# A GNN and mixture-of-experts layer on one core: sort matmuls interleaved, table rows every second group, four more dense tiles, x1 reloads on ScalarE's queue

## The chip, the cores and the metric

The program runs on one core of a Trainium2 chip. The metric is the device time of one execution in microseconds (us), median of the runs. Engines are named as the profile names them: PE (TensorE matmuls) and PEld (its weight loads), DVE (VectorE), ACT (ScalarE), POOL (GpSimd), SP (SyncE, which here only issues DMAs). A "q" behind a name is that engine's sequencer issuing something.

## What is computed

A graph layer with 12,500 nodes of 256 features and 212,500 weighted edges, then a mixture of 8 experts of which each node uses 2:

```python
def _L0_gnn_ref(x, W, bias, edge_row, edge_col, edge_val):
    h = x @ W
    msgs = h[edge_col] * edge_val[:, None]
    return jax.ops.segment_sum(msgs, edge_row, num_segments=N_NODES) + bias

def _L0_ffn_ref(x, gamma, beta, Wr, br, W1, b1, W2, b2):
    xn = layernorm(x) * gamma + beta
    top_vals, top_idx = jax.lax.top_k(xn @ Wr + br, 2)
    w_full = softmax(top_vals) placed at top_idx
    for e in range(8):
        h = jax.nn.gelu(xn @ W1[e] + b1[e])
        y = y + (h @ W2[e] + b2[e]) * w_full[:, e]
    return y

x = x + _L0_gnn_ref(_layernorm(x), W, bias, src, dst, edge_weight)
x = x + _L0_ffn_ref(_layernorm(x), ...)
```

## The kernel before

Nodes are in 98 tiles of 128 rows. Each engine has its own program; they meet at semaphores, and every engine works strictly in the order written. The work has these stages.

1. **Counts and places** (0 to 390 us): for each tile of nodes, how many edges fall to it, and where each edge goes in a sorted list.
2. **Sort** (390 to 903 us): 64 groups of 26 columns of 128 edges. For group g, PE turns the digits of the edge places (`turn_digits`, L1776), multiplies them into distances in 7 parts (`distances`, L1785), ACT makes one-hots of each part by an exponential (`one_hots`, L917), DVE builds the values (`build`, L1342 to L1348), and PE spreads the 26 columns into the order of the list (`spread`, L1796, with four small matmuls of row numbers, L1801). The distances pass through two PSUM banks in turn, so PE may be at most two parts ahead of ACT. PE does distances(g) and then spread(g - 1). Every fourth group DVE (`records`) and ACT (`weights_of`) write a batch of 16 x 128 records, and POOL stores them with 16 indirect DMAs (`scatter`, L766). In POOL's program scatter(B) stands at group 4B + 6.
   Beside this, the table h of normalised x times W is made, one tile of rows at a time ("rows"). A step k of it is on PE L1720 and L1728 (`rows_of_h`), on ACT L861, L862, L867 and L851 (`rows`), on POOL L751 (`low_rows`, the low half of the 16-bit split) and two DMAs of SP. `step1`, `step2`, `step3` say at which points the 99 steps stand; `step3` holds the last 28 and puts them at groups 0 to 27 of the sort. Buffers are two deep: ACT's step for tile t waits until POOL has done `low_rows` of tile t - 2 and its store has landed (semaphores s_hhl and s_hst). low_rows(t) itself waits for ACT's step.
3. **Gather** (908 to 3345 us): POOL gathers rows of h for units of 8 x 128 edges (L798, 8 indirect DMAs each, 232 units), DVE makes targets (L1392 to L1403), PE sums them into the tile (L1832, L1834). After each tile follow layer norm, router and top-2. Tiles are "dense" or "routed". Sets of SB = 4 dense tiles (tiles 8c to 8c + 3, 12 sets, NSET) run through all 8 experts, one expert a step of the loop (`hidden`, L1885, 24 matmuls of 512 columns; `expert`, L1902, 48 of 256 columns), set c in steps 8c + 4 to 8c + 11; NEX = 96 such passes. The other 50 tiles (NR) are routed: ACT stores x1 (the rows so far) to `out` and the normalised rows to `z_rows`.
4. **Exchange** (3381 to 3478 us): SP reloads z rows (L691), POOL scatters each routed tile twice, once for each chosen expert (L815), in part 0 (the first R0 = 33 routed tiles) and later part 1. SP fills the ends of the experts' blocks with zeros (`fill_of`, L593 and L596, 9 DMAs) after DVE has set `zero_b` (L1648, L1649, which stand behind DVE's whole loop; s_rest), and then loads blocks (`load_block`, L703).
5. **Blocks** (3478 to 3917 us): NBL = NR + 2 x 8 = 66 blocks of 256 rows: `turn` (L1954), `first_layer` (L1970), `second_layer` (L1982, L1987), 54 matmuls in all for a block; ACT L1034, L1044, L1045; DVE L1663 to L1677; ACT stores the block to ys (L1052). From three blocks after the end of part 0 on, two routed tiles are combined with each block: POOL reloads x1 (L828, a plain DMA) and gathers two rows of ys for each node (L830), DVE combines (L1684, L1687), ACT stores to out (L1057).
6. **Tail** (3917 to 3980 us): the tiles of part 1 are combined the same way once all blocks are stored.

Of the kernel before, what the change touches and what calls it, by code (L numbers as in the profile page):

```python
# [5 lines left out]
def gnn_moe_layer_kernel(  # L6
# [115 lines left out]
    with ctx:  # L122
# [420 lines left out]
        step3 = {g: len(step1) + len(step2) + g for g in range(NT + 1 - len(step1) - len(step2))}  # L543
# [182 lines left out]
        def _(pool):  # L726
# [91 lines left out]
            for j in range(NR):  # L818
# [17 lines left out]
        def _(act):  # L836
# [113 lines left out]
            def transposed(t):  # L950
                act.wait_ge(s_tr, t + 1)
                reached(act, s_lgm, t - 1)
                q, c = t % (2 * SB), t // (2 * SB)
                dense = t not in place_of
# [34 lines left out]
            def store_set(c):  # L989
                act.wait_ge(s_yadd, SB * (quad(c * NE + NE - 1) + 1))  # L990
                if c == 0:
                    act.dma_start(out[0:P - PAD, :], acc[PAD:P, 0, 0, :]).then_inc(s_ost, 16)
                    r, q = P - PAD, 1
                else:
                    r, q = c * 2 * SB * P - PAD, 0
# [12 lines left out]
            for t in range(NT + SB - 1):  # L1008
# [11 lines left out]
                if t < NT:  # L1020
                    transposed(t)
                    if t % (2 * SB) == SB - 1 and t // (2 * SB) < NSET:
                        exps(t // (2 * SB))
# [56 lines left out]
        def _(dve):  # L1080
# [367 lines left out]
            def epilogue(t):  # L1448
                dense = t not in place_of
                q, c = t % (2 * SB), t // (2 * SB)  # L1450
# [15 lines left out]
            def x_low(t):  # L1466
                q, c = t % (2 * SB), t // (2 * SB)
# [4 lines left out]
            def top2(t):  # L1472
                dense = t not in place_of
                q = t % (2 * SB)
# [126 lines left out]
            def step(t):  # L1601
# [20 lines left out]
                if t < NT:  # L1622
# [5 lines left out]
                    elif t % (2 * SB) == SB - 1:  # L1628
                        differences(t // (2 * SB))
                        finalise(t // (2 * SB))  # L1630
# [14 lines left out]
            for t in range(NT + SB + 1):  # L1645
# [63 lines left out]
        def _(pe):  # L1709
# [69 lines left out]
            def distances(g):  # L1779
                pe.wait_ge(s_seen, slot_of_turn(g) + 1)  # L1780
                for j in range(NCH):
                    n, w = slot_of_part(g, j), width_of(j)
                    if n >= 2:
                        pe.wait_ge(s_seen, n - 1)
                    nc.tensor.matmul(slot(n)[:, 0:w * P], digits_T[:, g % 2, :],  # L1785
# [251 lines left out]
```

## Time and profile before

| | us |
|---|---|
| median of 3 runs (3973.16 to 3984.31) | 3982.83 |
| profiled execution | 3981.84 |
| its span, first to last instruction | 3979.7 |
| PE busy | 3194.3 (80%) |
| POOL busy | 2538.3 (64%) |
| DVE busy | 2415.8 (61%) |
| ACT busy | 1331.0 (33%) |

The span is 2.1 us shorter than the profiled execution's time, and that time is 1.0 us below the median. Busy shares are averages over six stages with different limits, so each stage has to be read by itself.

The views are read so. The table of stretches has, for each window in us, the busy time and the number of instructions of PE, PEld, DVE, ACT and POOL, PE's granted clock (1.00 is 2.4 GHz, 0.50 is 1.2 GHz), the DMA share and GB/s. A row of waits says who waited for whom, us in total, times, longest. A row of the groups has line, engine, operation, tiles, count, busy us and mean ns, then the idle time before them and what ended it. A row of the timeline has start us, us, engine, line, operation, tiles and count, with the idle time before it in brackets. A row of one line's instructions has count, shortest/median/longest ns, first and last start. A POOL row's DMA_INDIRECT is the making of one indirect DMA, not its transfer.

### The profile page before, as it was taken

The numbers are of one execution on the slowest core, as the hardware profiler recorded it, in microseconds if no ns is written. First come the engines' busy times: TensorE is split into PE (matmuls) and PEld (weight loads), VectorE is DVE, ScalarE is ACT, GpSimd is POOL, SyncE is SP. The second block draws the span as 40 slices with busy tenths as digits, with TensorE's granted clock in tenths as the row PEclk, the third lists the DMA queues.
The fourth block names the chain that finished last, engine by engine and source line by source line (L and its number), as shares of the span: only waits on it lengthen the run. The fifth ranks groups of instructions, "written<-read, shape, count | busy, mean of one in ns | idle before, by whom it ended". The sixth has DMA issues, their size and how long they took to land.

```text
span 3979.7 us, 75949 instructions
## 1 busy us (share of the span) xinstructions
PE 3194.3 (80%) x20888; PEld 2076.7 (52%) x20888; DVE 2415.8 (61%) x6037; ACT 1331.0 (33%) x2857; POOL 2538.3 (64%) x2491
## 2 busy tenths in 40 slices
PE   6677767824788899898988998998988989099983
PEld 4444444412455555555555555555555556088862
DVE  9699334514666666666666666676666665144563
ACT  1354656720222222222222222222222222066651
POOL 1241457877777777777777777777777776630264
PEclk9899989966899999999999999999999999599996
DMA  4341110003434334434343434343334346552463
GB/s 154 106 117 60 33 36 15 8 12 92 117 110 119 110 113 114 119 112 120 112 117 110 117 110 120 109 115 108 114 111 120 108 118 104 175 165 86 125 202 113
DMA packets 288427, 420.20 MB, mean 106 GB/s; under 512 B 89733, under 2 KB 218314, under 8 KB 288138
## 3 DMA queue, kind: packets, MB, share of 16 engines
q0 software_dynamic: 109280, 279.33, 25.2%
q1 hardware_dynamic: 112536, 72.81, 6.4%
q10 hardware_dynamic: 66324, 64.42, 5.1%
q8 instruction: 157, 2.57, 0.3%
q14 instruction: 130, 1.06, 0.1%
HBM read 339.36 MB, written 76.98 MB: 105 GB/s over the span
## 4 chain that ended last, share of the span: by engine, by line
PE 36%; DVE 14%; issue 11%; POOL 7%; DVEq 5%; DMA 2%; ACT 1%; SPq 1%; ACTq 0%; POOLq 0%
PE twin L1902 7%; PE twin L1832 6%; PE bank L1902 6%; POOL area L798 5%; DVE area L1395 3%; PE twin L1834 3%; DVEq L1410 2%; DVE area L1403 2%; PE twin L1885 2%; PE bank L1885 2%; PE twin L1970 2%; PE twin L1987 2%; POOL zs L815 2%; PE bank L1970 1%; PE bank L1987 1%
## 5 line engine op out<-in xcount | busy, mean ns | idle before, releaser
L798 POOL DMA_INDIRECT area<-h_table,listed x1856 | 1864.3, 1004 | 606.0 <-issue 542.9
L1832 PE MATMUL twin<-area 128*128 x2608 | 880.9, 385 | 76.7 <-POOLq L797 38.3
L1834 PE MATMUL twin<-area 128*128 x2608 | 718.2, 275 | 0.0
L973 ACT ACTIVATE area<-twin,b_t 128x512 f32<-128x512 f32 x192 | 132.0, 687 | 1446.0 <-PE twin L1885 860.2
L1403 DVE TENSOR_TENSOR area<-area,listed 128x1024 f16 x652 | 422.6, 689 | 106.9 <-DVE area L1395 94.9
L1832 PEld LDWEIGHTS twin<-area 128*128 x2608 | 257.0, 99 | 415.2 <-issue 183.3
L766 POOL DMA_INDIRECT edge_list<-area,didx x256 | 313.0, 1223 | 77.1 <-issue 77.1
L1902 PE MATMUL twin<-w2h,area 128*128 128x256 f16 x1536 | 338.6, 317 | 0.0
L751 POOL TENSOR_TENSOR area<-area 128x256 f16<-128x256 f32 x98 | 80.9, 829 | 339.8 <-ACT area L862 339.6
L1834 PEld LDWEIGHTS twin<-area 128*128 x2608 | 257.1, 99 | 49.1 <-issue 0.2
L1902 PE MATMUL bank<-w2h,area 128*128 128x256 f16 x1536 | 267.7, 273 | 0.0
L1785 PE MATMUL twin<-area 128*128 128x512 f16 (+1 forms) x448 | 173.0, 392 | 113.7 <-ACT area L909 65.9
L1392 DVE TENSOR_SCALAR rel<-listed,tile_no 128x8 f16 x326 | 77.8, 239 | 297.9 <-issue 251.0
L1510 DVE TENSOR_TENSOR area<-area 128x512 f16<-128x512 f32 x384 | 244.0, 688 | 17.2 <-ACT area L975 17.2
L1902 PE MATMUL twin<-w2l,area 128*128 128x256 f16 x768 | 243.7, 317 | 0.0
L1395 DVE TENSOR_TENSOR area<-pair_no,rel 128x1024 f16<-128x1024 f16 x326 | 225.7, 692 | 11.2
L917 ACT ACTIVATE area<-twin 128x512 f16<-128x512 f32 (+1 forms) x448 | 228.9, 565 | 5.5 <-PE twin L1785 5.2
L1885 PE MATMUL twin<-area,w1h 128*128 128x512 f16 x768 | 229.5, 380 | 0.0
L1885 PE MATMUL bank<-area,w1h 128*128 128x512 f16 x768 | 228.8, 380 | 0.0
L1851 PE MATMUL bank<-ident,zb 128*128 128x128 f32 x196 | 44.9, 316 | 207.7 <-DVE zb L1446 207.4
L1671 DVE TENSOR_TENSOR area<-area 128x512 f16<-128x512 f32 x132 | 91.4, 692 | 197.8 <-ACT area L1045 197.8
L828 POOL DMA_DIRECT2D area<-out_dram x50 | 29.3, 586 | 285.5 <-issue 220.6
(339 smaller groups left out, 6505.3 us busy)
## 6 DMA issues: line engine op xcount, KB each, us to landing
area<-h_table,listed POOLq DMA_INDIRECT x1856
area<-in_x_dram SPq DMA_DIRECT2D x194, 128.0 KB, 2.2
area<-zs SPq DMA_DIRECT2D x66, 256.0 KB, 2.9
ys<-area ACTq DMA_DIRECT2D x66, 256.0 KB
out_dram<-area ACTq DMA_DIRECT2D x100, 128.0 KB, 2.6
h_table<-area SPq DMA_DIRECT2D x97, 128.0 KB, 1.7
xt<-in_x_dram ACTq DMA_DIRECT2D x97, 128.0 KB
area<-in_L_ffn_W_dram ACTq DMA_DIRECT2D x16, 512.0 KB, 4.0
```

What stands on the lines that cost most here:

```text
L766: pool.indirect_dma_start(out=list_v, out_offset=bass.IndirectOffsetOnAxis(ap=didx[B % 4][:, j, r:r + 1], axis=0), in_=record[:, B % 4, j, ...
L798: pool.indirect_dma_start(out=stage[:, (k % RU) * UNIT + 2 * D * c:(k % RU) * UNIT + 2 * D * (c + 1)], out_offset=None, in_=h_table[:, :], ...
L917: nc.scalar.activation(ohs[:, g % 2, PER * j:PER * j + w, :].rearrange("p c s -> p (c s)"), slot(n)[:, 0:w * P], ACT.Exp, scale=SHARP).the ...
L973: nc.scalar.activation(h32[:, m, :], psH[m][:, :], ACT.Gelu, scale=1.0 / WSCALE, bias=b1_t[:, e * KH + m:e * KH + m + 1])
L1395: nc.vector.tensor_tensor(equal[:, :, :, :], pair_no[:, :, :].unsqueeze(1).to_broadcast([P, RUN // 2, P, 2]), rel[:, :].rearrange("p (j e) ...
L1403: made = nc.vector.tensor_tensor(target[:, ds((i % TR) * TGT + part * (TGT // 2), TGT // 2)].rearrange("p (j s e) -> p j s e", j=RUN // 2, ...
L1510: nc.vector.tensor_tensor(hl[:, i % 2, m, :], h32[:, m, :], hh[:, i % 2, m, :], ALU.subtract).then_inc(s_hl, 1)
L1785: nc.tensor.matmul(slot(n)[:, 0:w * P], digits_T[:, g % 2, :], rh[:, PER * j:PER * j + w, :].rearrange("p c s -> p (c s)"), start=True, st ...
L1832: nc.tensor.matmul(psA[:, :], target[:, ds(at, P, 2)], stage[:, ds(rows, 2 * D)], start=False, stop=False)
L1834: last = nc.tensor.matmul(psA[:, 0:D], target[:, ds(at + TGT // 2, P, 2)], stage[:, ds(rows, D)], start=False, stop=False)
L1885: last = nc.tensor.matmul(psH[m][:, :], a, r, start=(k == 0 and n == 0), stop=(k == KD - 1 and n == 2))
L1902: last = nc.tensor.matmul(half_bank(q), a, r[:, e, m, :], start=(m == 0 and n == 0), stop=(m == KH - 1 and n == 2))
```

## The change

Four edits. In the sort PE no longer does all 7 parts of the distances of group g and then all 26 columns of spread(g - 1); after each of the parts 1 to 6 it does four or five of those columns, and the four small matmuls (`places_of`) at the end. The last 28 table steps stand at the even groups 0, 2, ... 54 in place of 0 to 27. The last four tiles, 94 to 97, become a 13th dense set: 52 dense tiles, 104 passes, 46 routed tiles, R0 = 30, NBL = 62; the set's eight passes are steps 100 to 107 of the loop, behind the last tile. And the x1 reloads of the routed tiles go from POOL's queue to ACT's: the first four ahead of the blocks, each later one right behind the store of the tile four before it.

```diff
-    NSET = NT // (2 * SB)
+    begins = list(range(0, NT - 2 * SB + 1, 2 * SB)) + [NT - SB]
+    NSET = len(begins)
+    set_of = {b + q: (c, q) for c, b in enumerate(begins) for q in range(SB)}
-    routed = [t for t in range(NT) if t % (2 * SB) >= SB or t >= 2 * SB * NSET]
+    routed = [t for t in range(NT) if t not in set_of]
...
-        step3 = {g: len(step1) + len(step2) + g for g in range(NT + 1 - len(step1) - len(step2))}
+        step3 = {2 * k: len(step1) + len(step2) + k for k in range(NT + 1 - len(step1) - len(step2))}
...
-                p = routed[j] % 2
                 if j >= RX:
                     pool.wait_ge(s_o, j - RX + 1)
-                pool.wait_ge(s_xst[p], 16 * len([t for t in routed[:j + 1] if t % 2 == p]))
-                pool.dma_start(xr[:, j % RX, :], out_rows(routed[j])).then_inc(s_xr[j % RX], 16)
...
-            for t in range(NT + SB - 1):
+            for t in range(NEX + SB):
...
+            def load_x1(j):
+                p = routed[j] % 2
+                act.wait_ge(s_xst[p], 16 * len([t for t in routed[:j + 1] if t % 2 == p]))
+                act.dma_start(xr[:, j % RX, :], out_rows(routed[j])).then_inc(s_xr[j % RX], 16)
+
             def store_out(j):
                 act.wait_ge(s_o, j + 1)
                 act.dma_start(out_rows(routed[j]), ot[:, j % RX, :]).then_inc(s_ofin[j % RX], 16)
+                if j + RX < NR:
+                    load_x1(j + RX)
+
+            for j in range(RX):
+                load_x1(j)
...
-            def distances(g):
-                pe.wait_ge(s_seen, slot_of_turn(g) + 1)
-                for j in range(NCH):
...
+            def distance(g, j):
+                n, w = slot_of_part(g, j), width_of(j)
+                if j == 0:
+                    pe.wait_ge(s_seen, slot_of_turn(g) + 1)
+                if n >= 2:
+                    pe.wait_ge(s_seen, n - 1)
...
+            def spread(g, columns):
                 h, B, j = g % 2, g // BATCH, g % BATCH
-                pe.wait_ge(s_build, g + 1)
-                pe.wait_ge(s_seen, slot_of_part(g, NCH - 1) + 1)
-                for c in range(GC):
+                if columns[0] == 0:
+                    pe.wait_ge(s_build, g + 1)
+                    pe.wait_ge(s_seen, slot_of_part(g, NCH - 1) + 1)
+                    if j == 0 and B >= 2:
+                        pe.wait_ge(s_wrec, B - 1)
+                for c in columns:
...
+            between = [range(GC * k // (NCH - 1), GC * (k + 1) // (NCH - 1)) for k in range(NCH - 1)]
...
-                distances(g)
+                distance(g, 0)
+                for j in range(1, NCH):
+                    distance(g, j)
+                    if g >= 1:
+                        spread(g - 1, between[j - 1])
                 if g >= 1:
-                    spread(g - 1)
+                    places_of(g - 1)
                 if g in step3:
                     rows_of_h(step3[g])
-            spread(NGRP - 1)
+            spread(NGRP - 1, range(GC))
+            places_of(NGRP - 1)
...
-            for t in range(NT + SB + 1):
+            for t in range(NEX + SB + 1):
```

The rest of the diff replaces the arithmetic `t % (2 * SB)`, `t // (2 * SB)` by the lookup `set_of` and `begins` in ACT's, DVE's and PE's steps.

## Rows read from the trace of the kernel before

**Rows 1.** Table of stretches: first half of the sort, the gather, the exchange

```profile
425.00:630.00 205.00, 135.86 (x1005) 88.07 (x1006) 67.66 (x109) 118.95 (x317) 117.00 (x102) 0.87 0.12 33
...
904.00:3345.00 2441.00, 2144.30 (x13039) 1328.38 (x13040) 1593.00 (x4468) 615.32 (x1093) 1847.15 (x1839) 0.95 0.40 113
...
3390.00:3474.00 84.00, 0.00 (x0) 0.00 (x0) 5.68 (x6) 0.85 (x2) 59.67 (x60) 0.50 0.51 172
```

**Rows 2.** Waits of POOL's own instructions, 446 to 903.5 us

```profile
POOL area L751 <- ACT area L862: 54.7, 11, 8.1
```

**Rows 3.** Groups of POOL: 446 to 658, 658 to 821.5, 821.5 to 903.2 us

```profile
L766 POOL DMA_INDIRECT edge_list<-area,didx x96 | 117.2, 1220 | 28.4 <-issue 28.4
...
L766 POOL DMA_INDIRECT edge_list<-area,didx x96 | 133.5, 1391 | 29.1 <-issue 29.1
...
L766 POOL DMA_INDIRECT edge_list<-area,didx x64 | 62.4, 974 | 19.5 <-issue 19.5
```

**Rows 4.** Two lines of DVE's build: L1348 from 658 to 821.5 us, L1342

```profile
L1348 DVE TENSOR_TENSOR area<-area x32: 1872/1880/1887, 659.3 to 818.6; 128x3328 f16<-128x3328 f16 x32
...
L1342 DVE TENSOR_TENSOR area<-pair_no,area x64: 582/592/1012, 388.2 to 817.8; 128x832 f16<-128x832 f16 x64
```

**Rows 5.** Timeline of POOL: first and last scatter of the sort, and between

```profile
446.25 1.15 POOL L766 DMA_INDIRECT edge_list<-area,didx  x1 [0.19 <-issue]
...
469.49 1.30 POOL L751 TENSOR_TENSOR area<-area 128x256 f16<-128x256 f32 x2
...
481.35 1.48 POOL L751 TENSOR_TENSOR area<-area 128x256 f16<-128x256 f32 x1 [7.95 <-ACT area L862]
...
902.18 0.96 POOL L766 DMA_INDIRECT edge_list<-area,didx  x1 [0.31 <-issue]
```

**Rows 6.** Timeline of ACT: a group with a table step, one without

```profile
423.73 3.64 ACT L917 ACTIVATE area<-twin 128x512 f16<-128x512 f32 x7
...
430.93 0.61 ACT L917 ACTIVATE area<-twin 128x512 f16<-128x512 f32 x1
...
694.10 3.52 ACT L917 ACTIVATE area<-twin 128x512 f16<-128x512 f32 x7
...
699.20 0.60 ACT L917 ACTIVATE area<-twin 128x512 f16<-128x512 f32 x1
```

**Rows 7.** Timeline, end of the expert passes: PE, and DVE's clearing of zeros

```profile
3370.61 0.59 PE L1885 MATMUL twin<-area,w1h 128*128 128x512 f16 x2
...
3381.03 0.27 PE L1902 MATMUL twin<-w2h,area 128*128 128x256 f16 x1
...
3388.05 0.91 DVE L1649 MEMSET area<- 128x1024 uint32 x1 [0.16 <-issue]
```

**Rows 8.** Timeline of the exchange: POOL's first scatter, SP's fills, loads, first block

```profile
3381.39 1.00 POOL L815 DMA_INDIRECT zs<-area,slot_i  x1 [7.88 <-DMA area<-h_table,listed]
...
3458.62 9.16 SPq L593 DMA_DIRECT2D zs<-area  x8
...
3471.50 2.98 SPq L703 DMA_DIRECT2D area<-zs  x3
...
3477.80 0.61 PE L1970 MATMUL twin<-area,w1h 128*128 128x256 f16 x2 [2.39 <-DVE area L1665]
```

**Rows 9.** Table of stretches: blocks without and with tiles being combined

```profile
3540.00:3740.00 200.00, 196.88 (x1757) 169.89 (x1755) 99.74 (x195) 128.62 (x328) 0.00 (x0) 1.00 0.28 86
3765.00:3895.00 130.00, 106.74 (x924) 90.92 (x922) 79.94 (x165) 67.19 (x172) 76.31 (x86) 0.97 0.62 188
```

**Rows 10.** Timeline of POOL in the tail: its first and last x1 reload

```profile
3920.44 0.57 POOL L828 DMA_DIRECT2D area<-out_dram  x1 [48.97 <-DMA ys<-area]
...
3971.41 0.59 POOL L828 DMA_DIRECT2D area<-out_dram  x1
```

**Rows 11.** The line of ACT's stores to out

```profile
L1057 ACTq DMA_DIRECT2D out_dram<-area x50: 338/466/2122, 3767.3 to 3977.5; - x50
```

**Rows 12.** DMA issues of the page: the store of the table, us to landing

```profile
h_table<-area SPq DMA_DIRECT2D x97, 128.0 KB, 1.7
```

More of the change, by code:

```diff
@@ L952, in transposed @@
                 reached(act, s_lgm, t - 1)
-                q, c = t % (2 * SB), t // (2 * SB)
-                dense = t not in place_of
+                dense = t in set_of
+                c, q = set_of.get(t, (0, 0))
                 if dense:
@@ L994, in store_set @@
                 else:
-                    r, q = c * 2 * SB * P - PAD, 0
+                    r, q = begins[c] * P - PAD, 0
                 act.dma_start(out[r:r + (SB - q) * P, :].rearrange("(q p) d -> p q d", p=P),
@@ L1021, in _ @@
                     transposed(t)
-                    if t % (2 * SB) == SB - 1 and t // (2 * SB) < NSET:
-                        exps(t // (2 * SB))
+                    if t in set_of and set_of[t][1] == SB - 1:
+                        exps(set_of[t][0])
             store_set(NSET - 1)
@@ L1448, in epilogue @@
             def epilogue(t):
-                dense = t not in place_of
-                q, c = t % (2 * SB), t // (2 * SB)
+                dense = t in set_of
+                c, q = set_of.get(t, (0, 0))
                 rows = acc[:, c % 2, q, :] if dense else accr[:, t % 2, :]
@@ L1466, in x_low @@
             def x_low(t):
-                q, c = t % (2 * SB), t // (2 * SB)
+                c, q = set_of[t]
                 dve.wait_ge(s_xTh, t + 1)
@@ L1472, in top2 @@
             def top2(t):
-                dense = t not in place_of
-                q = t % (2 * SB)
+                dense = t in set_of
+                c, q = set_of.get(t, (0, 0))
                 biggest, which = (mx[:, q, :], ix[:, q, :]) if dense else (mxr[:, :], ixr[:, :])
@@ L1777, in turn_digits @@
                                  start=True, stop=True).then_inc(s_made, 1)
-            def distances(g):
-                pe.wait_ge(s_seen, slot_of_turn(g) + 1)
-                for j in range(NCH):
[L1782 to L1785, printed above, removed]
-                                     rh[:, PER * j:PER * j + w, :].rearrange("p c s -> p (c s)"), start=True,
-                                     stop=True).then_inc(s_made, 1)
-            def spread(g):
-                h, B, j = g % 2, g // BATCH, g % BATCH
-                pe.wait_ge(s_build, g + 1)
-                pe.wait_ge(s_seen, slot_of_part(g, NCH - 1) + 1)
-                if j == 0 and B >= 2:
-                    pe.wait_ge(s_wrec, B - 1)
-                for c in range(GC):
+            def distance(g, j):
[4 more added lines that the diff above has]
+                    pe.wait_ge(s_seen, n - 1)
+                nc.tensor.matmul(slot(n)[:, 0:w * P], digits_T[:, g % 2, :],
+                                 rh[:, PER * j:PER * j + w, :].rearrange("p c s -> p (c s)"), start=True,
+                                 stop=True).then_inc(s_made, 1)
+            def spread(g, columns):
+                h, B, j = g % 2, g // BATCH, g % BATCH
+                if columns[0] == 0:
[4 more added lines that the diff above has]
+                for c in columns:
                     nc.tensor.matmul(ps_out[B % 2][:, j * NF * Q:(j + 1) * NF * Q], ohs[:, h, c, :],
@@ L1798, in spread, with places_of @@
                                      stop=(c == GC - 1))
+            def places_of(g):
+                h, B, j = g % 2, g // BATCH, g % BATCH
                 for r in range(RQ):
@@ L1906, in weights_T @@
             def weights_T(c):
-                t = c * 2 * SB + SB
+                t = begins[c] + SB
                 pe.wait_ge(s_wf, c + 1)
@@ L1926, in _ @@
             pe.wait_ge(s_clear, 1)
-            for t in range(NT + SB + 1):
+            for t in range(NEX + SB + 1):
                 i = t - SB
```

6 lines of the change are left out of this document (3 added, 3 removed).

## The prediction

> **What bounds the kernel now.** I read the stretches of the timeline first, because the whole-span shares hide that every stage has another limit, and then the waits and the timeline of the engine that each stretch points to.
>
> The gather is 2441 of 3980 us. POOL is busy 1847 us of it with the making of indirect DMAs [rows 1], with 0.3 us of issue before each as in the sort [rows 5]; it never rests for long, and the change doesn't touch it. So its length is taken as it is, and the ends are what counts: when it starts and what is left behind it.
>
> It starts when the last scatter of the sort has landed, so the sort ends with POOL: last call at 902.18 [rows 5], though PE, ACT and DVE finish their groups at about 825. In the first half POOL has 117 busy us in 205 [rows 1]. It waits 54.7 us, in 11 waits, for ACT's table step [rows 2]. The timeline shows why: a batch of 16 scatters starts at 446.25, low_rows follow at 469.49, and the low_rows that stands ahead of the next batch starts only at 481.35 after 7.95 us of waiting [rows 5]. It is a ring. low_rows is queued behind 16 scatters, ACT's step two tiles on waits for it, the groups behind that step wait too, and the next batch waits for the groups. In the second half nothing waits but POOL is full: 96 calls take 133.5 busy and 29.1 idle [rows 3], 1.69 us each. After the groups end, a call takes (62.4 + 19.5) / 64 = 1.28 us [rows 3]. The 39.7 us by which 96 calls are longer fall on 32 builds of DVE [rows 4], 1.24 us each.
>
> Behind the gather, PE has nothing to do from 3390 to 3474 and its clock is at 0.50, 1.2 GHz [rows 1]: it waits for POOL's scatters of part 0 and then SP's fills and loads [rows 8]. Then come 66 blocks, bound by PE (196.9 of 200 us busy, [rows 9]), and a tail bound by POOL [rows 10].
>
> **Part 1, the sort.** What the change gives here I sum as POOL's own time. When does POOL start? Now a group with a table step takes 430.93 - 423.73 = 7.20 us and one without 699.20 - 694.10 = 5.10 [rows 6]. ACT's exponentials are 3.52 of it, the rest is ACT waiting until PE has done the spread. With the columns between the parts that wait goes: PE's 26 columns and 7 parts fit beside ACT's exponentials. The nearest rows give the bounds for a group without a table step: 3.52 us (the exponentials alone) and today's 5.10; I take 4.1, near the lower, because each part must still pass from PE to ACT. For one with a step, 6.5 (7.20 is the bound above). Before the first batch stand six groups; three lose their table step (3 x 3.1) and three gain 0.7: 446.25 - 11.4 = 435.
>
> From there on I have to ask whether POOL still waits. A step at every second group halves the demand, and two tiles back now means four groups back. ACT's step at group 4B + 6 needs only the low_rows ahead of scatter(B - 1), which is done before that batch starts; the first step that needs one behind scatter(B - 1) is that of group 4B + 8. So scatter(B) is ready some 15 us after scatter(B - 2) ends (0.65 of low_rows, a store that lands 1.7 us after its issue [rows 12] and ACT's step, about 4 us; then two groups of 10.6 us together), while scatter(B - 1) keeps POOL busy for 25 us. The ring is open with 10 us to spare, and POOL is full from 435 on. The sum: 435 + 256 calls x 1.28 (328) + 57 builds x 1.24 (71) + 12 pairs of low_rows x 1.4 (17; 1.30 a pair [rows 5], and 0.1 at the handover) = 851. Today 903: 52 us less. In bounds: 35 less if the groups keep 7.2 and 5.1 and clock dips cost more, 60 less if builds that now fall in POOL's waits cost nothing. Note what this says of the interleaving: it only brings the start forward. The groups need about 22 us a batch, POOL 28; even at 24.6 (two of each kind as today) POOL would be the bound.
>
> The columns add no wait of their own: the build and the last exponential of group g - 1 are done one group earlier than they are asked for. Table stores end at group 54, long before 851. The gather starts 52 us earlier, with everything behind it.
>
> **Which price a build has is where the Trainium skill comes in.** Calls beside builds are 0.42 us longer on average [rows 3], and I take 1.24 us for a build. The Trainium skill, page "SBUF — State Buffer", section "Who interferes with whom", says that VectorE and GpSimd share one pair of ports, that a VectorE instruction with two SBUF inputs can hold off GpSimd, and that the loser is blocked for the whole instruction. This is a rule against packing builds beside scatters; what it would give here is the third rival.
>
> **Part 2, the thirteenth set.** It adds eight passes. hidden of the last pass starts at 3370.61, expert of the last at 3381.03 [rows 7]: one pass is 10.42 us of PE at full clock. Eight are 83.4, and weights_T with b2_terms add about 2, a clock dip or two 2 more: 87.4. They stand where PE was idle. But DVE's zeros (done at 3388.96, [rows 7]) stand behind its whole loop, and SP's fills wait for them. They were covered: fills started only at 3458.62, after SP had fed POOL's scatters of part 0 [rows 8]. Part 0 is now 60 scatters and not 66: 3381.4 + 60 x 1.28 = 3458, no longer last. Zeros are now done at 3388.96 + 87.4 = 3476.4, which is late next. From the first fill to the first block's matmul there are 3477.80 - 3458.62 = 19.2 us [rows 8], all in series: nine fills, landing, load, turn. So the first block starts at 3476.4 + 19.2 + 0.3 = 3495.9: 18 us later than now. Bounds: 14 (fewer clock dips) and 27 (clock at half for a while, or the set's exponentials and table loads holding up passes at steps 97 and 98).
>
> **Blocks.** 54 matmuls a block: 1757 / 54 = 32.5 blocks in 200 us, 6.15 each, and 924 / 54 = 17.1 in 130, 7.60 each, while tiles are combined [rows 9]. Part 0 has three tiles fewer, so of four blocks saved two are of each kind: 2 x 6.15 + 2 x 7.60 = 27.5.
>
> **Part 3, reloads on ACT.** A DMA issue costs ACT 0.34 to 0.47 us [rows 11]. While tiles are combined ACT's last store waits for DVE's last combine and the next gelu waits for that store, so ACT is on the path. The first of two reloads fits into ACT's wait for the second combine; the second adds 0.45 to each of 15 blocks: 6.8 us. Bounds: 0, and 15 if both count. The first four reloads (1.7 us) stand beside SP's fills. In the tail POOL starts its x1 reloads (3971.41 - 3920.44) / 16 = 3.19 us apart [rows 10], two gathers and a reload to a tile. Without the reload two gathers take 2.56, and there are 16 tiles, not 17: 16 x 2.56 = 41.0 against 16 x 3.19 + 3.4 = 54.4. That is 13.4 less; the last landing, combine and store stay. Bounds: 8 and 15.
>
> **Sum**, against the profiled execution's 3981.8: -52 + 18 - 27.5 + 6.8 - 13.4 = -68.1, so 3913.7, and 1.0 more for the median: 3914.7, say 3915.
>
> **Rivals.** *The ring stays closed (the slower side).* If ACT's step at group 4B + 6 still depended on a low_rows behind the previous batch, for instance because the store of that tile lands late, each of 12 batches would have a gap of about 13.4 us (16 scatters end at 469.5, the next batch begins at 483) and not 1.4, and there were five such gaps till now. That is 144 us more, less some 26 for builds that fall into the gaps: 3915 + 118 = 4033. It decides at a gap of 7 us a batch (3915 + 12 x 5.6 = 3982). Against it speak the 10 us of room. Chance 6%.
>
> *Only part of it.* ACT and PE don't get from 7.2 and 5.1 to less, clock dips and record batches fall together, and POOL is left with gaps of 4 us, or a build costs more. The sort then gives 25 us and not 52, and the first block is 25 us late and not 18: 3915 + 27 + 7 = 3949. Chance 14%.
>
> *A build blocks POOL for its whole length.* A build's long step is 1.88 us, with its first step of 0.59 [rows 4] it would be 2.47 and not 1.24: 57 x 1.23 = 70 more, 3985, no faster than now. By the rule named above this is what would come. The trace has 32 builds at 1.24, so 3%.
>
> *The blocks or the tail take back the gain* (ACT's queue holding its gelus up by more than both issues, as the 2.1 us of the longest store [rows 11] would): 15 blocks x 1.7 = 25 more than reckoned, 3940. Chance 7%.
>
> **How the numbers follow.** The forecast case has 70%. Its own range is the bounds together, not all at one end: 3897 to 3936. Reaching to the two partial cases gives 3896 to 3950; outside are the closed ring, the blocked POOL and some of each tail. A measurement of this kernel can tell 0.3%, 12 us. Faster by more than that: 70 + 14 + 7 less 3 for what the two partial cases may come to = 88%. Within 0.3%: 5%. Slower: 7%.
>
> **What would show it.** In the changed profile: no waits of POOL L751 for ACT L862 beyond a few us between the first and last scatter; first scatter near 435, last near 851; in a group without a table step the L917 starts 4.1 us apart; PE busy at full clock from 3390 - 52 on for some 85 us; nine fills starting right behind DVE's zeros, not behind the scatters; first block 18 us later counted from the first gather; 62 blocks, 8.05 us each while tiles are combined; gathers of ys in the tail 1.28 us apart with nothing between. I am wrong if POOL has gaps in the sort, if passes without a tile take much more than 10.4 us, or if ACT's store and reload pairs spread the blocks further.

## The result and the profile after

| | before | after |
|---|---|---|
| median, us | 3983.57 (4 runs) | 3913.78 (4 runs, 3908.99 to 3914.66) |
| profiled execution, us | 3981.84 | 3912.91 |
| its span, us | 3979.7 | 3911.1 |
| POOL busy, us | 2538.3 (64%) | 2494.5 (64%) |

The kernel before is the one run beside it. After divided by before is 0.9828, 95% interval 0.9809 to 0.9846: 69.8 us less. 3915 was forecast. Seven of the twelve experiments below ran where the kernel before took 5333 to 5362 us, its gather above all being slower; their totals tell little, and only their stages are read. The span cut at the points which the prediction named:

| stretch | before | after | difference | predicted |
|---|---|---|---|---|
| start to first gather | 907.9 | 855.7 | -52.2 | -52 |
| first gather to the first block's matmul | 2569.9 | 2580.5 | +10.6 | +18 |
| first block's matmul to the last of all | 439.3 | 422.6 | -16.7 | -20.7 |
| last matmul to the end | 62.6 | 52.3 | -10.3 | -13.4 |
| sum | 3979.7 | 3911.1 | -68.6 | -68.1 |

The first term and the sum are right to half a us; the three terms behind it are off by 3 to 7 us, one in the change's favour and two against it. The rows now. First the table of stretches after (us, then busy us and instructions of PE, PEld, DVE, ACT, POOL, clock, DMA share, GB/s): the sort, the added passes, blocks without and with tiles being combined.

```profile
425.00:630.00 205.00, 147.55 (x1292) 101.58 (x1291) 98.52 (x150) 147.83 (x380) 166.20 (x133) 0.89 0.11 27
3330.00:3414.00 84.00, 83.69 (x593) 58.19 (x590) 36.25 (x68) 35.28 (x56) 57.52 (x58) 1.00 0.42 139
3500.00:3700.00 200.00, 196.77 (x1753) 169.40 (x1752) 100.61 (x197) 127.80 (x326) 9.70 (x10) 1.00 0.30 93
3702.00:3831.10 129.10, 100.56 (x810) 83.26 (x810) 71.14 (x146) 58.93 (x151) 46.58 (x49) 0.92 0.58 173
```

POOL's busy time in the same 205 us of the sort went from 117.00 [rows 1] to 166.20. The passes keep PE busy for 83.69 of 84 us at full clock. While tiles are combined, 810 matmuls at 54 a block are 15 blocks in 129.1 us, 8.61 each (7.60 in [rows 9]).

The waits of POOL after, 430 to 855 us (us in total, times, longest):

```profile
POOL edge_list L768 <- issue: 74.7, 247, 0.3
POOL area L753 <- ACT area L861: 8.7, 1, 8.7
```

The waits of [rows 2] are gone but for one, which ends before the first scatter. The timeline of POOL shows the same at the places of [rows 5]: first scatter, low_rows directly between two batches, last scatter, first gather.

```profile
428.79 1.48 POOL L753 TENSOR_TENSOR area<-area 128x256 f16<-128x256 f32 x1 [8.72 <-ACT area L861]
430.45 1.16 POOL L768 DMA_INDIRECT edge_list<-area,didx  x1 [0.18 <-issue]
...
455.24 1.76 POOL L768 DMA_INDIRECT edge_list<-area,didx  x1 [0.30 <-issue]
457.02 1.32 POOL L753 TENSOR_TENSOR area<-area 128x256 f16<-128x256 f32 x2
458.50 1.15 POOL L768 DMA_INDIRECT edge_list<-area,didx  x1 [0.16 <-issue]
...
850.03 0.96 POOL L768 DMA_INDIRECT edge_list<-area,didx  x1 [0.31 <-issue]
855.73 0.98 POOL L800 DMA_INDIRECT area<-h_table,listed  x1 [4.74 <-SPq L677]
```

The first twelve batches start 27.2 to 28.1 us apart, with 1.5 us between the last call of one and the first of the next. ACT's exponentials, to be held against [rows 6]:

```profile
685.89 3.52 ACT L916 ACTIVATE area<-twin 128x512 f16<-128x512 f32 x7
...
691.85 3.64 ACT L916 ACTIVATE area<-twin 128x512 f16<-128x512 f32 x7
696.10 3.52 ACT L916 ACTIVATE area<-twin 128x512 f16<-128x512 f32 x7 [0.29 <-PE twin L1794]
705.66 0.38 ACT L860 ACTIVATE area<-bank 128x256 f16<-128x256 f32 x1 [6.04 <-DMA h_table<-area]
```

A group with a table step is 691.85 - 685.89 = 5.96 us, one without 4.25. Then ACT waits 6 us for a store whose low_rows stand behind the batch in POOL's order: once in four groups ACT waits for POOL, and POOL no longer for ACT. From the 17th to the 52nd the groups start about 11.0, 6.0, 6.0 and 4.3 us apart in turn, together POOL's 27.3 a batch.

### The profile page after: what moved, and what is told of

It is laid out like the page before. It is cut to its first block, busy times and chain, and to the rows that moved or that the text cites. A ratio compares the mean times of both kernels' runs of the same rounds, so it can differ in the third digit from the quotient of the medians.

```text
span 3911.1 us, 76490 instructions
## 1 busy us (share of the span) xinstructions
PE 3228.5 (83%) x21249; PEld 2117.9 (54%) x21249; DVE 2439.0 (62%) x6051; ACT 1362.3 (35%) x2894; POOL 2494.5 (64%) x2425
## 4 chain that ended last, share of the span: by engine, by line
PE 43%; DVE 16%; issue 9%; DVEq 5%; POOL 3%; DMA 1%; ACT 1%; ACTq 0%; SPq 0%; POOLq 0%
PE twin L1922 9%; PE bank L1922 7%; PE twin L1852 7%; DVE area L1404 4%; PE twin L1854 3%; PE twin L1905 3%; PE bank L1905 3%; DVEq L1419 2%; POOL area L800 2%; PE twin L1990 2%; DVE area L1412 2%; PE twin L2007 2%; PE bank L1990 2%; PE bank L2007 1%; DVE rel L1401 1%
## 5 line engine op out<-in xcount | busy, mean ns | idle before, releaser
L972 ACT ACTIVATE area<-twin,b_t 128x512 f32<-128x512 f32 x208 | 142.9, 687 | 1468.6 <-PE twin L1905 821.8
L768 POOL DMA_INDIRECT edge_list<-area,didx x256 | 326.4, 1275 | 76.2 <-issue 74.7
L1922 PE MATMUL twin<-w2h,area 128*128 128x256 f16 x1664 | 355.2, 311 | 0.0
L829 POOL DMA_INDIRECT area<-ys,back_i x92 | 89.3, 971 | 334.4 <-DMA ys<-area 260.4
L1519 DVE TENSOR_TENSOR area<-area 128x512 f16<-128x512 f32 x416 | 266.7, 689 | 48.9 <-ACT area L974 48.9
L1922 PE MATMUL bank<-w2h,area 128*128 128x256 f16 x1664 | 289.5, 273 | 0.0
L1922 PE MATMUL twin<-w2l,area 128*128 128x256 f16 x832 | 258.3, 310 | 0.0
L1905 PE MATMUL twin<-area,w1h 128*128 128x512 f16 x832 | 247.9, 380 | 0.0
L1905 PE MATMUL bank<-area,w1h 128*128 128x512 f16 x832 | 247.6, 379 | 0.0
L1922 PE MATMUL bank<-w2l,area 128*128 128x256 f16 x832 | 226.9, 273 | 0.0
```

Of the source, the lines that this page charges most:

```text
L768: pool.indirect_dma_start(out=list_v, out_offset=bass.IndirectOffsetOnAxis(ap=didx[B % 4][:, j, r:r + 1], axis=0), in_=record[:, B % 4, j, ...
L1519: nc.vector.tensor_tensor(hl[:, i % 2, m, :], h32[:, m, :], hh[:, i % 2, m, :], ALU.subtract).then_inc(s_hl, 1)
L1905: last = nc.tensor.matmul(psH[m][:, :], a, r, start=(k == 0 and n == 0), stop=(k == KD - 1 and n == 2))
L1922: last = nc.tensor.matmul(half_bank(q), a, r[:, e, m, :], start=(m == 0 and n == 0), stop=(m == KH - 1 and n == 2))
```

## What the experiments showed

**Which edit gives what.** Four kernels did one edit each on the kernel before, whose median beside them was 3977.55 (19 runs).

*Only the interleaving* (`distance`, `spread(g - 1, between[j - 1])` and `places_of` as in the diff of the change; the table steps left at groups 0 to 27).

> The kernel before with only the spread columns put between the parts of the distances; table steps at groups 0 to 27, 12 sets, reloads on POOL. My theory (the ring of low_rows, ACT's step and scatter limits the first half, POOL the second): the ring stays closed, with five waits of POOL; the groups get about 1.2 us shorter, so the first scatter comes some 7 us earlier and each of the five gaps of 13.4 us shrinks to about 10; last scatter near 880 (903 before), time 20 to 24 us less. Rival (the interleaving is what frees POOL): last scatter near 851, 50 us less. Rival (POOL full anyway in the second half): only the first scatter's 7 us.

Measured: 3972.21, ratio 0.9986 (0.9977 to 0.9996), 5.3 us less. First scatter 436.7 (446.25 before), last ending at 894.2 (903.1): what was won ahead of the first scatter, 9.6 us, was kept (8.9), and nothing more. Its waits of POOL, 436 to 895 us:

```profile
POOL edge_list L766 <- issue: 76.7, 255, 0.3
POOL area L751 <- ACT area L862: 49.5, 11, 7.7
```

Eleven waits, as before, with 49.5 us and not 54.7: faster groups don't open the ring, and what its waits lost, 5.2 us, the calls took back: they are 69.5 us over 0.97 each in all, and 64.7 before, since more of them stand beside builds. I had written 20 to 24 us less and was wrong; the prediction's own sentence, that interleaving "only brings the start forward", was right.

*Only the rows.*

```diff
-        step3 = {g: len(step1) + len(step2) + g for g in range(NT + 1 - len(step1) - len(step2))}
+        step3 = {2 * k: len(step1) + len(step2) + k for k in range(NT + 1 - len(step1) - len(step2))}
```

> The kernel before with only the last 28 table steps at groups 0, 2 ... 54. My theory: this alone opens the ring. POOL is full from the first scatter (about 440, three of six groups at 5.1 us and not 7.2) to the last near 857; gaps between batches 1.5 us and not 13.4; time some 46 us less. A group pair takes 12.3 us, 24.6 a batch, which is less than POOL's 27. Rival (PE and ACT must be faster too, or else the ring only moves): gaps of 5 us and more stay, last scatter at 880 or later.

Measured: 3936.51, ratio 0.989 (0.9873 to 0.9906), 41.0 less, last scatter ending at 858.9. So this one line opens the ring. I had expected groups of 24.6 us a batch and gaps of 1.5 us; the groups take 7.2 and 6.5 us in turn, 27.4 a batch, and there are 3.9 us between POOL's batches of 23.4: the groups are the bound, at the same 27.3 us a batch at which POOL is when both edits are made. Added to this line, the interleaving brings the first scatter from 439.3 to 430.4 and the last from 858.9 to 851.0, and moves nothing between.

*Only the thirteenth set* (`begins`, `set_of`, loops to NEX + SB).

> The kernel before with only the thirteenth dense set. My theory, with the sizes that the changed kernel showed: first block 10 us later counted from the first gather, 62 blocks and not 66 (27.5 us less), the 4.8 us stall at the tenth block gone, one tile less in the tail (3.2 us less): 25 us less, about 3958. Rival (the stall's end belongs to another edit): 20 us less.

Measured: 3958.18, ratio 0.9941 (0.9924 to 0.9957), 19.4 less. First block 2584.4 us after the first gather, against 2569.9: 14.5 later, and not 10. From it to the last matmul there are 408.2 us, 31.1 less: four blocks, and the step from the ninth block to the tenth, 6.2 us and not 10.9. So the end of that stall belongs to this edit. I had expected 25 us less in all.

*Only x1 on ACT's queue.*

> The kernel before with only the x1 reloads on ACT's queue. My theory as the changed kernel showed it: each of 17 blocks with tiles being combined takes 1.0 us more (8.6 and not 7.6), the 17 tiles of the tail 0.6 us less each: 17 - 10 = 7 us MORE, about 3990. Theory of the prediction (0.45 us a block): 7.6 - 10 = 3 us less, about 3981.

Measured: 3988.3, ratio 1.0019 (1.0009 to 1.0028): 10.8 us more by the medians, 4 to 11 by the interval. Alone this edit is a loss. Its own part is nearer to 7, as expected: in the profile 3.4 of 10.8 us more lie ahead of the first gather, which the edit doesn't touch, while first block to last matmul takes 13.5 more and the rest 6.4 less. The stretches with tiles being combined, of the set alone (reloads on POOL) and of this kernel (on ACT), columns as above:

```profile
3759.90:3875.00 115.10, 95.50 (x811) 81.06 (x812) 71.20 (x146) 59.20 (x151) 65.81 (x75) 0.96 0.63 190
```

```profile
3766.60:3912.80 146.20, 117.66 (x918) 96.34 (x919) 79.91 (x164) 66.92 (x171) 52.81 (x55) 0.89 0.56 170
```

15 blocks at 7.67 us and 17 at 8.60: the edit costs 0.93 us a block (0.96 against the 7.64 of the same 17 blocks before), two issues of 0.47 us [rows 11]. Both count.

By the medians the four edits alone come to 54.9 us less, and together they gave 69.8. By the stages of the profiles, counting for each edit those that it touches, they nearly add up: sort -8.9 and -44.2, first block +14.5, blocks -31.1 and +13.5, tail -3.2 and -6.4, which with 0.3 in e4's gather is -65.5 against -68.6. Most of the rest is the gather's own length (2467.9 us of calls in e3_set_only, 2463.6 in the changed kernel). So no edit needs another one to be worth what it is.

**x1 reloads on SP's queue.** The changed kernel with

```diff
-                act.dma_start(xr[:, j % RX, :], out_rows(routed[j])).then_inc(s_xr[j % RX], 16)
+                sp.dma_start(xr[:, j % RX, :], out_rows(routed[j])).then_inc(s_xr[j % RX], 16)
...
+                for j in combined_by(n - 5):
+                    if j + RX < NR:
+                        sp.wait_ge(s_o, j + 1)
+                        load_x1(j + RX)
```

The lower lines stand behind SP's load of block n; the first four reloads behind its first block loads.

> The changed kernel with the x1 reloads of the routed tiles on SP's queue instead of ACT's (the first four behind the loads of the first blocks, each later one behind a block load). Theory (both issues of ACT count in every block in which tiles are combined, 1.0 us together): these blocks go from 8.5 back to 7.6 us, 15 blocks, so 14 to 15 us less than the changed kernel: 3899, ratio to the kernel before about 0.979. Rival (a block is 8.5 us for another reason, such as POOL's gathers now being back to back): blocks stay at 8.5 and the time at 3914. In the tail the distance from the last combine to the end stays near 5.4 us by the theory that POOL's own end is last there, and falls to 2 to 3 us if it is ACT's queue.

The total, 5328.6 against 5332.59, ratio 0.9981 (0.9948 to 1.0015), tells nothing. In the stage, the 15 blocks with tiles combined took 8.23 us each, and 8.87 in e7_build_in_4 and 8.95 in e6_zeros_early beside it with reloads on ACT. Where the kernel before took 3978 us, the same edit, with others ahead of the blocks, gave 7.61 (e13, below), with POOL's gathers still back to back: so the gathers aren't what made these blocks longer. From the last gather of the tail to the end there were 9.3 us, exactly as with reloads on ACT (3901.87 to 3911.1): so not ACT's queue but POOL ends last.

**The zeros early.** DVE's two clearings moved from behind its loop to its step NT + 4:

```diff
+                if t == NT + 4:
+                    dve.wait_ge(s_idle, 1)
+                    nc.vector.memset(zero_b, 0.0)
+                    nc.vector.memset(b2_z, 0.0).then_inc(s_rest, 1)
```

> The changed kernel with DVE's two clearings that the fills wait for moved from behind DVE's loop into its step 102, before the last passes of the experts end. Theory (DVE's place in the order is what ends last ahead of the fills): the first fill starts some 60 us earlier, as soon as SP is done with the scatters' reloads, and the first block starts when the next late thing lets it, which I take to be DVE's weights and ACT's exponentials behind the loop, or PE's own last pass: 3425 instead of 3436, 11 us less, 3903. Rival (the chain fills, landing, load, turn is not what the first block waits for): nothing changes, 3914.

Total 5321.61 against 5332.59, ratio 0.9977 (0.9943 to 1.001). As expected, 11.8 us went: first block at 4813.9, 10.6 us behind PE's last pass, where the changed kernel has 22.4 (3413.8 to 3436.2). The timeline of DVE and PE shows what is late next:

```profile
4810.23 2.33 DVE L1672 TENSOR_TENSOR area<-area 1x2048 f16<-1x2048 f32 x1
4812.59 0.43 DVE L1676 CAST area<-area 128x512 f16<-128x512 f32 x1
4813.06 0.69 DVE L1678 TENSOR_TENSOR area<-area 128x512 f16<-128x512 f32 x1
...
4813.89 0.60 PE L1994 MATMUL twin<-area,w1h 128*128 128x256 f16 x2 [10.19 <-DVE area L1678]
```

The split of b2, 5 us of DVE behind its loop, stands ahead of the first block's cast. That was never on the path before, since fills were later.

**Both, and all of the preparation early.** x1 on SP, the clearings at step 102, weights and b2 at 107, ACT's exponential and table load at 101. It was run three times.

> The changed kernel with x1 reloads on SP's queue and with all preparation of the blocks early: DVE's clearings at its step 102, the weights and b2 at 107, ACT's exponential and table load at 101. Theory: 15 us from the reloads, 11 us from the clearings and up to 8 more as the first block then waits for PE's last pass and its own load alone (3417): 3880 to 3888. Rival (the early instructions take DVE's or ACT's time from the last passes): the passes stretch by 3 to 5 us and the time is 3890 to 3900.

Measured: 5306.71 against 5332.59, ratio 0.9959 (0.9928 to 0.999). First block 3.8 us behind the last pass, the passes not stretched.

> The kernel of e8_sp_and_early once more, since its chip took 5333 us for the kernel before, over a thousand more than the others, with runs 80 us apart, so that only stages could be read there. From those stages: first block 3.8 us behind the last pass of PE and not 22.4 (18.6 less), blocks with tiles combined 8.1 us and not 8.7 (9 to 15 us less in all). On a chip like that of the changed kernel's runs that is 3914 - 18.6 - 12 = 3883. Rival (what is won ahead of the blocks is given back in the first ten, where SP's queue mixes block loads and reloads of z): 3895 to 3905.

Measured: 5307.82 against 5362.27, ratio 0.9906 (0.9874 to 0.9938); again 3.8 us.

> The kernel of e9_sp_and_early_again a third time, since all comparisons after the first ran where the kernel before took over 5330 us. Where it takes about 3980 the theory gives 3914 - 18.6 (first block 3.8 us and not 22.4 behind the last pass of PE) - 14.5 (15 blocks with tiles combined at 7.64 us and not 8.61) = 3881, first block 22 to 24 us earlier against the first gather's start than 2580.5, no more than 2563; the end still 9.3 us behind the last gather's issue. Rival (the first blocks give it back, as in e8 and e9, where the blocks 2 to 5 took 46 us and not 25): 3900. Where the kernel before takes over 5300 us again: ratio 0.99 to 0.996 as before, and nothing new.

Measured: 3883.91, kernel before 3978.38, ratio 0.9759 (0.9743 to 0.9776). It is faster than the changed kernel by about 0.7%, the two intervals lying apart, and its profiled span is 30.1 us shorter (3881.0). First block 2561.9 us after the first gather, 18.6 earlier, the term of the expectation's sum and not the 22 to 24 that it also names. Its first block and the stretch with tiles combined:

```profile
3418.12 0.39 PE L2004 MATMUL twin<-area,w1h 128*128 128x256 f16 x2 [3.34 <-DVE area L1688]
```

```profile
3687.70:3801.80 114.10, 93.96 (x810) 80.29 (x810) 70.80 (x146) 58.94 (x151) 47.80 (x49) 0.97 0.65 195
```

15 blocks at 7.61: 15.0 us less than at 8.61. But the tenth block began 12.9 us behind the ninth and not 6.2, which gives back 6.7. What holds it up is SP's queue: the tenth block's load stands behind five rounds of three z rows, one z row and nine fills; here it went out 51.9 us behind the first block's matmul, and 48.2 in the changed kernel (52.3 before). SP, here first and then the changed kernel:

```profile
3415.45 2.77 SPq L712 DMA_DIRECT2D area<-out_dram  x4
...
3470.01 5.03 SPq L706 DMA_DIRECT2D area<-zs  x5
```

```profile
3484.41 12.18 SPq L705 DMA_DIRECT2D area<-zs  x6
```

The four first x1 reloads, 2.8 us of SP, stand ahead of these rounds, and the blocks start sooner against them. That these are the reasons is read from the order; neither was tried alone.

**What a build costs a scatter.** In the changed kernel's trace, DVE and POOL in the same stretch:

```profile
604.32 1.89 DVE L1357 TENSOR_TENSOR area<-area 128x3328 f16<-128x3328 f16 x1
607.51 0.59 DVE L1351 TENSOR_TENSOR area<-pair_no,area 128x832 f16<-128x832 f16 x1 [1.30 <-PE twin L1814]
...
608.33 1.87 DVE L1357 TENSOR_TENSOR area<-area 128x3328 f16<-128x3328 f16 x1
```

```profile
603.07 0.97 POOL L768 DMA_INDIRECT edge_list<-area,didx  x1 [0.31 <-issue]
604.34 2.70 POOL L768 DMA_INDIRECT edge_list<-area,didx  x1 [0.30 <-issue]
607.35 0.96 POOL L768 DMA_INDIRECT edge_list<-area,didx  x1 [0.30 <-issue]
608.62 2.42 POOL L768 DMA_INDIRECT edge_list<-area,didx  x1 [0.31 <-issue]
```

The call of 604.34 ends at 607.04, the build's at 606.21; the call of 608.62 at 611.04, the build's at 610.20: 0.84 us after it, and so do all 54 calls of the trace that start while L1357 runs (0.83 to 0.85). A call that is undisturbed takes 0.97 us, so it has 0.13 us behind it when it is stopped and then does the rest. Calls that started up to 0.18 us before the build were held too in the kernel before, those that started 0.25 us or more before it were not. The shorter L1351 (L1342 before) holds calls the same way:

```profile
433.07 0.59 DVE L1351 TENSOR_TENSOR area<-pair_no,area 128x832 f16<-128x832 f16 x1 [3.33 <-PE twin L1814]
```

```profile
433.19 1.32 POOL L768 DMA_INDIRECT edge_list<-area,didx  x1 [0.30 <-issue]
```

L1351 ends at 433.66 and the call at 434.51, 0.85 us behind it. But it is short: 15 calls of this trace lost 1.7 us to it together, 24 calls before lost 6.3. A call comes every 1.28 us, so the wait for L1357 would be its length less half of that if they met at random, an estimate: 1.88 - 0.64 = 1.24. That this is the price read from [rows 3] is in part chance. Of the time lost there 4.6 us are the short instruction's and 36.1 the long one's, 1.13 a build; in the changed kernel the long one took 76.3 us for 56 builds, 1.36 each.

If so, shorter pieces should cost less. First four in a row:

```diff
-                nc.vector.tensor_tensor(rhs[:, h, :, :, :, :], ...)
+                for i in range(4):
+                    a, b = GC // 2 * i // 4, GC // 2 * (i + 1) // 4
+                    ins = nc.vector.tensor_tensor(rhs[:, h, a:b, :, :, :], ...)
```

> The changed kernel with the build's 1.88 us instruction cut into four of about 0.5 us each, the same work. Theory (a call of POOL that starts while such an instruction runs is held until this instruction ends, so that its price is its length less about half a call's period, 1.24 us): four short pieces let calls in between, the price falls to 0.3 to 0.6 us a build, the last scatter ends at 805 to 820 instead of 851, and the time is 30 to 45 us less: 3870 to 3885. Rival A (POOL stays out until all pieces have ended): last scatter at 851, time 3914. Rival B (the price is a matter of the bytes that DVE moves, not of the length of one instruction): each piece costs a quarter, the sum stays, 851.

Total 5343.05 against 5332.59, ratio 1.0001 (0.9969 to 1.0033). Last scatter ending at 864.9, and at 860.4 and 857.1 in two kernels beside it without the cut (e5_x1_on_sp, e6_zeros_early). So rival A holds: POOL stays out until all pieces have ended. DVE and POOL at one build:

```profile
537.29 2.08 DVE L1360 TENSOR_TENSOR area<-area 128x768 f16<-128x768 f16 x4
```

```profile
537.58 2.63 POOL L768 DMA_INDIRECT edge_list<-area,didx  x1 [0.30 <-issue]
```

Four pieces of 0.55 us take 2.08, so each begins before the last has ended, and the call ends at 540.21, 0.84 us behind the fourth. Then the same pieces apart, on top of the kernel with all preparation early:

```diff
+                    if i:
+                        dve.wait_ge(s_seen, slot_of_part(g, 2 * i - 1) + 1)
```

> The kernel of e9_sp_and_early_again with the build's instruction cut into four, of which the second, third and fourth each wait for ACT's exponential of the parts 1, 3 and 5 of the same group, so that they stand about 1.2 us apart; in e7_build_in_4 the four followed each other so closely (each started before the one before had ended) that they held POOL as one of 2.1 us. Theory (a call that reaches its port while such an instruction runs waits until it ends, then needs 0.84 us more; so a lone piece of 0.55 us costs 0.55 / 1.28 x 0.55 / 2 = 0.12 us on average): the price of a build falls from 1.24 to about 0.5, 57 x 0.75 = 43 us less, last scatter at 808 to 815 instead of 851, time 38 to 43 us below that of e9. Rival A (what counts is the work that DVE does in all, not how long it holds on without a break): last scatter at 851 or later, time as e9. Rival B (the later end of the build makes PE wait for it and the groups slow down): groups above 5.5 us each, last scatter between 820 and 860.

```profile
538.67 0.69 DVE L1367 TENSOR_TENSOR area<-area 128x1024 f16<-128x1024 f16 x1 [2.31 <-issue]
...
541.70 0.55 DVE L1367 TENSOR_TENSOR area<-area 128x768 f16<-128x768 f16 x1
```

```profile
538.79 1.42 POOL L783 DMA_INDIRECT edge_list<-area,didx  x1 [0.30 <-issue]
540.51 0.97 POOL L783 DMA_INDIRECT edge_list<-area,didx  x1 [0.30 <-issue]
541.78 1.31 POOL L783 DMA_INDIRECT edge_list<-area,didx  x1 [0.30 <-issue]
```

The rule holds for single pieces (539.36 to 540.21, 542.25 to 543.09: 0.85 and 0.84), and the price fell: all 256 calls together were 15 us over 0.97 us each, and 81 in e9_sp_and_early_again, without the spacing. Most batches took 20.5 to 21.5 us. Yet the last scatter ended at 926.7 and the time was 5364.09 against 5362.27, ratio 0.9981 (0.9935 to 1.0027), 56 above e9. POOL's waits, 430 to 927 us:

```profile
POOL area L768 <- ACT area L877: 117.5, 14, 13.1
```

Rival B, and more than it: groups took some 8 us, and POOL waits for ACT's table step again.

> The kernel of e11_build_apart once more. On its chip the price of a build did fall (from 73 us over all calls to 15), but the last scatter came at 927, since groups took 8 us and more: ACT's exponentials started up to 2.2 us after they could have, where in the changed kernel's own trace they never waited over 0.4 us for PE; in the same chip's run without the spacing they waited up to 1.6. Theory (that delay belongs to that chip, whose kernel before took 5362 us): on a chip where the kernel before takes about 3980, the groups stay below 5.5 us, last scatter at 805 to 825, time 3914 - 19 (early preparation) - 12 (reloads on SP) - 30 to 40 (price of builds) = 3843 to 3855. Rival (the loop is in the order: DVE waits for ACT, PE for DVE): groups 6.5 us and more on any chip, last scatter 880 to 930, time 3910 to 3960. On the slow chip again: as e11_build_apart.

Measured: 5337.51 against 5334.81, ratio 1.0011 (0.9978 to 1.0043), last scatter ending at 928.0, as in the run before. It fell again on a slow kernel before, so whether the order itself (DVE waits for ACT's parts, PE for the build) slows the groups, or only there, stays open. What is shown is the price of a build, and that this way of lowering it isn't free.

## Why the prediction was right, point by point

**Sort, -52 predicted, -52.2.** The mechanism is shown: the ring opened, and rows alone open it. The start was 430.4 and not 435, because a group is 5.96 and not 6.5 with a table step (4.25 and not 4.1 without). From there on the trace gives 851.0 - 430.4 = 420.6 against 328 + 71 + 17 = 416. The calls together are 79 us over 0.97 us each, which makes 1.38 and not 1.24 for each of 57 builds, low_rows with handovers take 17 us as reckoned, and calls and issues by themselves 325 and not 328. The start came 4.6 us early and the rest was 4.6 us longer, so that the two meet at 851 is luck to that extent. One aside was wrong: "even at 24.6 POOL would be the bound". Without interleaving the groups take 27.4 (e2), since one without a step then takes 6.5 and not 5.10.

**Build beside scatter.** The third rival is out: 1.38 us a build with its short instruction, not 2.47. But the Trainium skill's rule (page "SBUF — State Buffer", section "Who interferes with whom", that the loser is blocked for the whole instruction) agrees with the rows: each call waits to the build's very end. My reading of it for the rival was wrong, not the rule: the price isn't the length but the length less the part that runs before a call gets there, for the short L1351 too. The same section holds, as inferred, that an instruction with two inputs leaves the making of descriptors alone; the 54 calls here say otherwise, and the measurement decides.

**First block, +18 predicted, +10.6.** The failed step is the term of the passes, "87.4". Zeros ended 79.5 us later against the first gather. From there to the first block it is 19.9 us, 19.5 predicted. Of the eight passes seven came 10.4 or 10.5 us behind the one ahead of them and one 12.5, at a clock of 1.00, without the dip allowed for. They took 85.6 us, 1.8 less than reckoned. What I didn't see is that the last passes of the kernel before weren't clean: `hidden` of the 94th, 95th and 96th began 13.4 and 12.1 us apart, where 10.42 was read from inside the last. After the change they begin 11.5 and 10.4 apart, and the 96th stands 4.1 us earlier against the end of the gather's calls (4.2 in e3_set_only). I take this for slack of the old tail which the added passes took up, but part of it belongs to that one trace: in e1, e2 and e4, without the set, the 96th stands 0.6 to 1.6 us earlier too. The last 2.0 are a gather that was shorter in this run, 2463.6 us of calls and not 2465.6; in e3_set_only it was 2467.9, hence +14.5 there.

**Blocks, -20.7 predicted, -16.7.** Four blocks are -27.6 by [rows 9], as reckoned. The step "The first of two reloads fits into ACT's wait for the second combine" was wrong: both issues count, 0.97 us a block, 14.5 and not 6.8 (e4 shows it with nothing else changed). It was offset by a thing that I hadn't reckoned: the step from the ninth block to the tenth took 10.9 us before and 6.2 after. With 46 routed tiles SP's last round of z rows holds one load and not two, and from its start to the tenth block's load there are 13.3 us and not 16.6. Together that is -17.8, and 1.1 us more is not accounted for. e3 has the same round and the same 6.2; e13 has the round too, but its other edits bring the stall back.

**Tail, -13.4 predicted, -10.3.** Two gathers take 2.59 us a tile, 2.56 predicted. "The last landing, combine and store stay" holds for these three: ACT is done 5.9 us behind the last gather's issue, before and after. What failed is that the program ends with them. The end comes 9.3 us behind the last gather's issue when gathers stand back to back, in every such run (9.3 in all nine kernels with the set and without reloads on POOL, 9.9 in e4), and 6.2 to 6.5 where an x1 reload stands between them (before, e1, e2, e3). In the trace the last thing is POOL's own closing step, 15.2 us long from 3895.7 to 3910.9, not ACT's store: ACT is done at 3907.8, and that gap of 3.1 us is the one by which the term is off. Before, POOL's step ended at 3978.5 and ACT at 3979.5. Why POOL's takes longer now wasn't tried.

So the total came out within a us only because mis-sized terms, 7.4 us one way and 4.0 and 3.1 the other, cancel. What carried it is the sort, whose mechanism and size both held.

## What to carry to other kernels

An engine that waits for its own earlier output through another engine's queue is a ring; count what stands between in each order, and change the spacing of the demand before making the steps faster: one line gave 41 us, the interleaving of PE 5 (9 in the profiles' sort). A DMA issue isn't free on an engine that is on the path, 0.47 us each, and moving it from the bound engine of the tail to one on the path of the blocks alone lost 13.5 us there and won 6.4; an engine that only issues DMAs is the place for it. When work is appended to a stage, look at what stands behind the loop of every engine, even where it was hidden so far: 18.6 us were to be had there.

## What the runs showed that I had not expected

Four instructions in a row on DVE hold POOL as one does: 2.08 us in place of 1.88, a call ending 0.84 us behind the last. In e11 the pieces stood apart, and calls got in between them.

The program's end is 9.3 us behind POOL's last indirect DMA where nothing but such calls stood ahead of it, since POOL's closing step then ends last, and 6.2 to 6.5 where x1 reloads stood between them.

The same kernel can take a third longer, nearly all of it in the gather. The changed kernel and e9_sp_and_early_again, 500 us of the gather, columns as above, then POOL's waits in the second:

```profile
1000.00:1500.00 500.00, 444.27 (x2734) 276.99 (x2735) 325.17 (x918) 128.95 (x228) 378.75 (x379) 0.95 0.40 114
```

```profile
1000.00:1500.00 500.00, 344.34 (x1753) 194.05 (x1754) 221.41 (x620) 76.49 (x141) 247.74 (x250) 0.79 0.27 75
...
POOL area L815 <- SPq L678: 186.4, 14, 20.3
```

250 gathers and not 379 in the same time. Of e9's 1399 us over e13, the same kernel, 1273 are the gather's calls and 84 lie between the last call and the last pass. The sort was 10 us longer. The blocks were not spared: first to last matmul took 443.9 us and not 411.5, most of it in the second to fifth block (46.5 us and not 24.3), and 8.16 us a block and not 7.61 while tiles were combined. One chip showed both at different times. The cause isn't known. What follows is that such a run's total can't be held against another's, and its stages only against those of runs beside it.
